# Address arithmetic and register loads moved to the front of each step, and a message sum put between the two halves of a later group's gathers

## The chip, the cores and the metric

One core of one Trainium2 chip runs the kernel. Its engines are the TensorE (PE in the profile, its weight loads PEld), the VectorE (DVE), the ScalarE (ACT), the GpSimd (POOL) and the SyncE (SP), which issues most DMAs. Each engine has a sequencer that reads its instructions in program order, works out register values itself, and hands matmuls, copies and the like on to the engine. The metric is device time in microseconds of one launch.

## The reference

A graph with 3125 nodes of 64 features and 100000 edges, sorted by destination. First a message network of three layers, then a relational network of three layers, each with a residual and a layer norm:

```python
for _ in range(3):                                   # message layers
    msg_in = jnp.concatenate([h[src], h[dst], edge_attr], axis=1)
    msg = silu(msg_in @ W1e + b1e) @ W2e + b2e
    agg = jax.ops.segment_sum(msg, dst, n) / deg
    h = h + mlp(jnp.concatenate([h, agg], axis=1), W1n, b1n, W2n, b2n)
...
for l in range(3):                                   # relational layers
    agg = segment_sum(x[src], edge_type * n + dst, 4 * n) / max(cnt, 1)
    x = x @ root + b + einsum('rni,rio->no', agg.reshape(4, n, -1), W)
```

## The kernel before

**Edges in groups.** The kernel first sorts the edges into tiles of 128 by their block of destination nodes and their span of source nodes (span of the first 1.35 ms, untouched by the change). Eight tiles (`GT = 8`) are a group, all with one destination block; there are `NG = 160` groups, and every one of the six layers goes over all of them. `places` holds, for every group, eight offsets into the table of source rows and, for the message layers, one more for the destination block.

**One step of the TensorE.** `stage(g, u, i)` is one step. The first four and the last few steps of a layer stand unrolled; the rest is a loop `Fori(1, QUADS)` of 39 passes with four steps in each, `u` being the number of the step within the pass. In the message layers (`l < LAYERS`, layers 0 to 2) a step holds: `gather_ready` (the group's one-hot matrices are there); `gather_tile` for eight tiles, three matmuls each (L934 and L935 pick the source rows out of two neighbouring parts of the table, L938 the destination row), 24 in all, into the four PSUM banks of `gat`; `turn_dst_hots`, eight transpositions of the destination one-hots (L948); `sum_messages` of the group three steps earlier, eight matmuls (L968); `load_places` for the next step (L916, nine registers out of SBUF). In the relational layers (`l >= LAYERS`, layers 3 to 5) it holds, for each of eight tiles, two gather matmuls and four sum matmuls (L977) of the group two steps earlier, 48 in all, with the load of eight registers (L918) after the fourth tile.

**Addresses.** The second operand of L934, L935 and L938 is `table_flat[:, bass.ds(register, K3)]`. Its address is worked out by the TensorE's own sequencer, in register records (`ISA` in the order, `FUSED_REGOPS` in the trace) that stand right ahead of the matmul that first needs them: two operations for L934, three for L935, two for L938, the last once a step.

**Waits.** `gat_read` says that the VectorE (the ScalarE in relational layers) has read half of `gat`; it is waited for ahead of tiles 0 and 4. The sum waits for `acc_read`, sent by the ScalarE's `keep_msums` (L714) two groups earlier, for `hot_out` (L693, the copy of the transposed one-hots), and for `low_made` of the GpSimd. On the ScalarE a step is `keep_hots` (L693, once `turned` says that the transpositions are done), `middle` (L707), `keep_msums` (L714), and `messages` (L701 and L702).

Of the kernel before, what the change touches and what calls it, by code (L numbers as in the profile page):

```python
# [18 lines left out]
GT = 8  # L19
# [3 lines left out]
K3 = 3 * HID  # L23
# [3 lines left out]
def gnn_kernel(nc, x, src, dst, edge_attr, edge_type, W1e, b1e, W2e, b2e, W1n, b1n, W2n, b2n,  # L27
# [22 lines left out]
    LAYERS = 3  # L50
# [19 lines left out]
    with ExitStack() as ctx:  # L70
# [46 lines left out]
        table_flat = table[:].rearrange("p b m k f -> p (b m k f)")  # L117
        table_next = table_flat[:, ROWW:]
# [668 lines left out]
        def _(pe):  # L787
# [100 lines left out]
            for l in range(2 * LAYERS):  # L888
# [93 lines left out]
                def stage(g, u, i, l=l):  # L982

                    known = isinstance(g, int)
                    gathers = not known or g < NG
                    off, dst_off = [], None
                    if gathers:
                        off = [pe.snap(r, min_val=0, max_val=SPAN * ROWW * (NS - 1)) for r in tile_regs[u % 2]]
                        if l < LAYERS:
                            dst_off = pe.snap(dst_reg[u % 2], min_val=0, max_val=ROWW * (NB - 1) + K3)  # L990
                        gather_ready(g, u, i)
                    if l < LAYERS:
                        if gathers:
                            for j in range(GT):
                                gather_tile(g, u, j, off, dst_off)
                            turn_dst_hots(g, u)
                        if not known or g >= LAG:
                            sum_messages(g - LAG, (u + 4 - LAG) % 4)
                        if gathers:
                            load_places(g + 1, u + 1)  # L1000
                    else:
                        adds = not known or g >= 2
                        for j in range(GT):
                            if gathers:
                                gather_tile(g, u, j, off, dst_off)
                            if adds:
                                if j == 0:
                                    sums_ready(g - 2, (u + 2) % 4)
                                sums_half(g - 2, (u + 2) % 4, j)
                            if j == 3 and gathers:  # L1010
                                load_places(g + 1, u + 1)

                load_places(0, 0)
                for g in range(4):
                    stage(g, g, 0)
# [432 lines left out]
```

## Time and profile before

| | us |
|---|---|
| median of 3 runs (lowest, highest) | 5863.55 (5863.24, 5865.77) |
| the profiled execution | 5864.59 |
| its span in the trace | 5862.9 |
| sorting of the edges and building of tables | 0 to about 1505 |
| message layer 0 | about 1505 to 2310 |
| message layers 1 and 2 | about 2350 to 3005, 3045 to 3705 |
| relational layers 3 to 5 | about 3745 to 5795 |

Busy shares of the span: PE 81%, PEld 69%, DVE 68%, POOL 58%, ACT 47%. The profile counts an engine's busy time by what the engine executes; time in which its sequencer works on registers is in no busy share, but the sequencer's records stand in the trace with the mark q (PEldq for the TensorE's). Columns of a group of instructions by line are: engine, operation, count, shortest/median/longest duration in ns, start of the first and of the last. "issue" is idle time for which the profile shows no releaser.

### The profile page before, as it was taken

To read this page: it belongs to the slowest core of one execution; us is meant where nothing else is said; L and a number is where in the kernel's file an instruction comes from. 1 tells how busy PE (TensorE), PEld (TensorE's weight loads), DVE (VectorE), ACT (ScalarE), POOL (GpSimd) and SP (SyncE) were. 2 spreads that over 40 slices of the span, in tenths; PEclk is the share of its full clock that TensorE was granted. 3 is DMA by queue.
4 is the path that set the end of the run, shared out by engine and by line. 5 is a ranking of instruction groups with operands and counts; after the bars stand their busy time and mean duration, and the time that the engine had idled before them with its cause. 6 is when DMAs were issued, how large, how long until landed. Compare 5 with 4: busy or idle time off the path is not lost.

```text
span 5862.9 us, 173813 instructions
## 1 busy us (share of the span) xinstructions
PE 4725.5 (81%) x47638; PEld 4058.5 (69%) x47639; DVE 3972.5 (68%) x9658; ACT 2755.2 (47%) x4407; POOL 3395.9 (58%) x4499
## 2 busy tenths in 40 slices
PE   2666666660577777888888888899999999999998
PEld 2444444440466665777767777699998999999997
DVE  6444444440589997777767777688875888578885
ACT  1111111112456665677757777555554555455553
POOL 0777777770367775455535555366653666446663
PEclk9755555555799999999999999899998999899997
DMA  8111111117899997777757777244432444234441
GB/s 327 29 29 29 29 29 29 29 28 244 272 312 333 334 334 245 248 264 266 264 176 265 263 265 265 92 133 133 132 120 83 132 132 133 93 109 133 132 133 58
DMA packets 358467, 975.41 MB, mean 166 GB/s; under 512 B 71168, under 2 KB 83796, under 8 KB 358411
## 3 DMA queue, kind: packets, MB, share of 16 engines
q1 hardware_dynamic: 317352, 946.00, 48.9%
q0 software_dynamic: 38400, 28.13, 2.7%
q10 hardware_dynamic: 2658, 0.51, 0.0%
q8 instruction: 37, 0.61, 0.0%
q14 instruction: 20, 0.16, 0.0%
HBM read 774.54 MB, written 199.06 MB: 166 GB/s over the span
## 4 chain that ended last, share of the span: by engine, by line
PE 56%; POOL 15%; issue 10%; DMA 9%; DVE 7%; another core or an unknown queue 2%; ACT 1%; DVEq 0%; POOLq 0%; SPq 0%; ACTq 0%
PE sums L977 21%; POOL recs L517 14%; PE gat L934 10%; PE gat L935 10%; DMA arena<-rows_d 5%; PE gat L938 4%; PE sums L968 4%; DMA arena<-recs 3%; PE sums L948 2%; DMA recs<-arena 2%; DVE arena L1341 1%; PE gat L1060 1%; DVE arena L1316 1%; DVE arena L1337 1%
## 5 line engine op out<-in xcount | busy, mean ns | idle before, releaser
L934 PE MATMUL gat<-table,arena 128*128 x7680 | 1913.4, 249 | 370.8 <-DVE arena L1341 186.7
L935 PE MATMUL gat<-table,arena 128*128 x7680 | 1916.7, 250 | 0.0
L977 PE MATMUL sums<-arena 128*128 128x192 bf16 x15360 | 1887.2, 246 | 0.0
L1357 DVE TENSOR_SCALAR arena<-iota_s,meta_t 128x512 bf16<-128x512 int16 x3840 | 1523.0, 469 | 363.2 <-PE sums L977 363.2
L977 PEld LDWEIGHTS sums<-arena 128*128 128x128 bf16 x15360 | 1325.3, 98 | 0.1
L517 POOL DMA_INDIRECT recs<-arena x800 | 949.8, 1187 | 377.4 <-issue 374.9
L721 ACT CAST arena<-gat 128x768 bf16<-128x768 f32 x960 | 767.0, 799 | 809.3 <-PE gat L935 809.3
L934 PEld LDWEIGHTS gat<-table,arena 128*128 128x128 bf16 x7680 | 747.7, 97 | 548.3 <-issue 482.1
L938 PE MATMUL gat<-table,arena 128*128 x3840 | 959.9, 250 | 0.0
L540 POOL TENSOR_TENSOR arena<-arena 128x512 bf16<-128x512 f32 x480 | 532.6, 1110 | 726.3 <-ACT arena L707 726.0
L1341 DVE TENSOR_TENSOR arena<-arena,gat 128x256 f32<-128x256 f32 x1920 | 812.0, 423 | 65.8
L935 PEld LDWEIGHTS gat<-table,arena 128*128 128x128 bf16 x7680 | 748.0, 97 | 137.2 <-issue 0.4
L592 POOL TENSOR_TENSOR arena<-arena 128x256 f32<-128x256 f32 x480 | 414.5, 864 | 656.7 <-ACT arena L729 655.9
L693 ACT COPY arena<-sums 128x1024 bf16<-128x1024 bf16 x480 | 486.3, 1013 | 518.2 <-PE sums L948 517.8
L1337 DVE TENSOR_TENSOR arena<-gat,arena 128x256 f32<-128x256 f32 x960 | 402.8, 420 | 263.4 <-PE gat L938 262.1
L832 PE MATMUL gat<-arena 25*125 25x39 bf16 x800 | 232.0, 290 | 401.8 <-DVE arena L1179 401.8
L656 ACT COPY arena<-gat 25x1000 bf16<-25x1000 bf16 x100 | 98.4, 984 | 829.8 <-PE gat L806 807.8
L832 PEld LDWEIGHTS gat<-arena 25*125 25x125 bf16 x800 | 141.2, 176 | 445.9 <-DVE arena L1179 429.7
L598 POOL TENSOR_TENSOR arena<-arena 128x256 f32 x480 | 384.6, 801 | 91.2 <-POOL arena L595 91.2
L968 PE MATMUL sums<-arena 128*128 128x192 bf16 (+1 forms) x3840 | 406.1, 248 | 11.1 <-ACT arena L714 10.9
L729 ACT COPY arena<-sums 128x768 f32<-128x768 f32 x480 | 386.2, 804 | 9.9 <-PE sums L977 9.9
L938 PEld LDWEIGHTS gat<-table,arena 128*128 128x128 bf16 x3840 | 380.3, 99 | 13.4
(184 smaller groups left out, 6228.6 us busy)
## 6 DMA issues: line engine op xcount, KB each, us to landing
arena<-hots_d SPq DMA_DIRECT2D x320, 768.0 KB, 4.5
arena<-hots_d SPq DMA_DIRECT2D x480, 512.0 KB, 3.5
arena<-recs SPq DMA_DIRECT2D x640, 272.0 KB, 3.9
hots_d<-arena SPq DMA_DIRECT2D x160, 768.0 KB, 8.1
arena<-rows_d SPq DMA_DIRECT2D x160, 512.0 KB, 6.9
recs<-arena SPq DMA_DIRECT2D x1, 43520.0 KB, 119.4
recs<-arena POOLq DMA_INDIRECT x800, 2.9
arena<-in_edge_attr_dram SPq DMA_DIRECT2D x100, 62.5 KB
```

Source lines behind the costliest of these rows:

```text
L517: pool.indirect_dma_start(recs, bass.IndirectOffsetOnAxis(ap=addr_out[s][:, j:j + 1].bitcast(U32), axis=0), rec_out[s][:, j, :], None).the ...
L540: pool.tensor_tensor(parts[u][:, :, 2 * HID:K3], left[s], parts[u][:, :, HID:2 * HID], ALU.subtract).then_inc(low_made, 1)
L693: act.copy(oh[u], oh_ps[u % 2].rearrange("p (j n) -> p j n", n=P)).then_inc(hot_out, 1)
L721: act.copy(gb[u % 4][:, 4 * h:4 * h + 4, :], gat[:, 1024 * h:1024 * h + 1024].rearrange("p (j w) -> p j w", j=4) [:, :, 0:K3]).then_inc(ga ...
L934: pe.matmul(at, ohT[u][:, 0, tile], table_flat[:, bass.ds(off[j], K3)], start=True, stop=False)
L935: ins = pe.matmul(at, ohT[u][:, 1, tile], table_next[:, bass.ds(off[j], K3)], start=False, stop=l >= LAYERS)
L938: ins = pe.matmul(at, ohT[u][:, 2, tile], table_flat[:, bass.ds(dst_off, K3)], start=False, stop=True)
L968: ins = pe.matmul(accp[u % 2][:, 0:w], oh[u][:, j, :], parts[u][:, j, 0:w], start=j == 0, stop=j == GT - 1)
L977: ins = pe.matmul(accp[s][:, 256 * r:256 * r + K3], oh4[u][:, t, r * P:(r + 1) * P], gb[u][:, t, :], start=t == 0, stop=t == GT - 1)
L1337: dve.tensor_tensor(z[s][:, tiles, :], found_parts[:, tiles, 0:HID], rec[:, tiles, 0:HID], ALU.add).then_inc(z_step, 1)
L1341: ins = dve.tensor_tensor(z[s][:, tiles, :], z[s][:, tiles, :], found_parts[:, tiles, m * HID:(m + 1) * HID], ALU.add)
L1357: ins = dve.tensor_scalar(oh4[u][:, j, :], iota_s[:], meta_t[:, bass.ds(GT * g + j, 1), PT - HID], None, ALU.is_equal)
```

## The change

In `stage`, all addresses of the step are now worked out at its front, by `pe.lower_ap` on the same operands; the matmuls then find them ready. In the message layers `load_places` for the next step follows at once, ahead of the group's wait and its gathers. And in the message layers the sum of group g - 3 stands after tiles 0 to 3; tiles 4 to 7 and the transpositions follow it. In the relational layers only the addresses move.

```diff
@@ in stage(g, u, i)
                         if l < LAYERS:
                             dst_off = pe.snap(dst_reg[u % 2], min_val=0, max_val=ROWW * (NB - 1) + K3)
+                            pe.lower_ap(table_flat[:, bass.ds(dst_off, K3)])
+                        for r in off:
+                            pe.lower_ap(table_flat[:, bass.ds(r, K3)])
+                            pe.lower_ap(table_next[:, bass.ds(r, K3)])
+                        if l < LAYERS:
+                            load_places(g + 1, u + 1)
                         gather_ready(g, u, i)
                     if l < LAYERS:
-                        if gathers:
-                            for j in range(GT):
+                        for j in range(GT // 2):
+                            if gathers:
                                 gather_tile(g, u, j, off, dst_off)
-                            turn_dst_hots(g, u)
                         if not known or g >= LAG:
                             sum_messages(g - LAG, (u + 4 - LAG) % 4)
                         if gathers:
-                            load_places(g + 1, u + 1)
+                            for j in range(GT // 2, GT):
+                                gather_tile(g, u, j, off, dst_off)
+                            turn_dst_hots(g, u)
```

TensorE, message layer 1, third step of a pass, before; the sum of the step ahead ends, the load and the copies of the registers follow, and then records and matmuls take turns:

```order
L968 MATMUL sums<-arena 128x192 x7
L916 ISA
L916 TENSOR_LOAD places
L988 ISA
L931 ISA [waits hots_loaded2]
L934 ISA [waits gat_read]
L934 MATMUL gat<-table,arena 128x192
L935 ISA
L935 MATMUL gat<-table,arena 128x192
L938 ISA
L938 MATMUL gat<-table,arena 128x192
```

The same place after; the transpositions now end the step ahead:

```order
L948 MATMUL sums<-ident_b,arena 128x128 x7
L988 ISA
L991 ISA
L994 ISA
L993 ISA x2
L994 ISA x3
L916 ISA
L916 TENSOR_LOAD places
L931 ISA [waits hots_loaded2]
L934 MATMUL gat<-table,arena 128x192 [waits gat_read]
L935 MATMUL gat<-table,arena 128x192
L938 MATMUL gat<-table,arena 128x192
```

So 17 address records of two or three operations each, spread over the step, have become seven of up to six operations in a row (L991, L994, L993 twice, L994 three times), and the wait for `gat_read` moved from a record to the matmul.

TensorE, relational layer 3, second step of a pass, before:

```order
L977 MATMUL sums<-arena 128x192 x4
L988 ISA
L931 ISA [waits hots_loaded1]
L934 ISA [waits gat_read]
L934 MATMUL gat<-table,arena 128x192
L935 ISA
L935 MATMUL gat<-table,arena 128x192
L954 REGISTER_ALU
L961 REGISTER_ALU [waits acc_read]
L977 MATMUL sums<-arena 128x192 [waits gat_read,oh_made]
```

and after:

```order
L977 MATMUL sums<-arena 128x192 x4
L988 ISA
L993 ISA
L994 ISA x3
L993 ISA x2
L994 ISA
L931 ISA [waits hots_loaded1]
L934 MATMUL gat<-table,arena 128x192 [waits gat_read]
L935 MATMUL gat<-table,arena 128x192
L954 REGISTER_ALU
L961 REGISTER_ALU [waits acc_read]
L977 MATMUL sums<-arena 128x192 [waits gat_read,oh_made]
```

Sixteen address records, two a tile, are now seven in a row ahead of the step's first matmul; the load of the registers (L918) keeps its place after the fourth tile.

## Rows read from the trace of the kernel before

**Rows 1.** Busy time by stretch: message layer 0, message layer 1, relational layer 3

```profile
core 0: us, PE busy (x) PEld busy (x) DVE busy (x) ACT busy (x) POOL busy (x), PEclk, DMA share, GB/s
1600.00:2200.00 600.00, 453.61 (x4948) 371.42 (x4949) 551.79 (x1238) 358.31 (x617) 427.21 (x739) 0.98 0.96 328
2400.00:2900.00 500.00, 441.67 (x4974) 357.50 (x4972) 382.84 (x870) 354.58 (x622) 283.47 (x499) 1.00 0.79 265
3800.00:4300.00 500.00, 500.00 (x6064) 500.00 (x6062) 403.77 (x1010) 289.96 (x379) 302.56 (x380) 1.00 0.42 132
```

**Rows 2.** TensorE's sequencer by line, 2380 to 3000 us (message layer 1)

```profile
L1016 PEldq COMPARE_BRANCH  x39: 76/208/221, 2382.0 to 2993.9; - x39
...
L916 PEldq FUSED_REGOPS  x153: 65/65/65, 2380.9 to 2992.8; - x153
L916 PEldq TENSOR_LOAD <-places x153: 836/843/867, 2381.0 to 2992.9; - x153
...
L988 PEldq FUSED_REGOPS  x114: 165/165/165, 2386.5 to 2989.9; - x114
...
L931 PEldq FUSED_REGOPS  x152: 46/46/60, 2382.7 to 2990.1; - x152
...
L934 PEldq FUSED_REGOPS  x1218: 37/37/42, 2380.1 to 2992.2; - x174
...
L935 PEldq FUSED_REGOPS  x1219: 46/51/56, 2380.0 to 2992.4; - x175
```

**Rows 3.** Order of time, PE alone, one step of message layer 1

```profile
2501.94 0.61 PE L948 MATMUL sums<-ident_b,arena 128*128 128x128 bf16 x8
2502.38 0.83 PE L968 MATMUL sums<-arena 128*128 128x192 bf16 x8
2503.57 0.25 PE L934 MATMUL gat<-table,arena 128*128 x1 [0.35 <-issue]
...
2505.82 0.28 PE L948 MATMUL sums<-ident_b,arena 128*128 128x128 bf16 x2
```

**Rows 4.** Line L916 in the same steps, 2501 to 2512 us

```profile
L916 PEldq FUSED_REGOPS  x3: 65/65/65, 2502.1 to 2509.8; - x3
```

**Rows 5.** Lines L934, L935 and L977, all that started between 3740 and 4101.92 us

```profile
L934 PEldq FUSED_REGOPS  x724: 42/42/42, 3747.1 to 4101.9; - x181
...
L934 PE MATMUL gat<-table,arena x721: 246/246/368, 3747.2 to 4101.9; 128*128 x181
...
L935 PE MATMUL gat<-table,arena x720: 246/246/368, 3747.3 to 4101.5; 128*128 x180
...
L977 PE MATMUL sums<-arena x2816: 242/246/246, 3753.6 to 4101.8; 128*128 128x192 bf16 x188
```

**Rows 6.** The loop's branch in relational layer 3, 3775 to 4378 us

```profile
L1016 PEldq COMPARE_BRANCH  x39: 76/208/215, 3775.8 to 4377.7; - x39
```

**Rows 7.** A record of six operations (GpSimd's), and loads of eight registers and of one

```profile
L582 POOLq FUSED_REGOPS  x120: 84/84/98, 3744.1 to 5781.2; - x120
...
L918 PEldq TENSOR_LOAD <-places x152: 588/592/598, 3778.0 to 4375.7; - x152
...
L547 POOLq TENSOR_LOAD <-places x480: 285/290/1572, 1543.9 to 3696.7; - x160
```

**Rows 8.** Order of time, ACT alone, the same step as in rows 3

```profile
2502.58 1.01 ACT L693 COPY arena<-sums 128x1024 bf16<-128x1024 bf16 x1 [1.19 <-PE sums L948]
2503.49 0.62 ACT L707 CAST arena<-arena 128x512 bf16<-128x512 f32 x1
2504.01 0.32 ACT L714 COPY arena<-sums 128x192 f32<-128x192 f32 x1
```

**Rows 9.** What TensorE sat idle for ahead of L968, whole span: us, times

```profile
  ACT arena L714: 23.1, 12
```

**Rows 10.** Branch and register load in message layer 0

```profile
L1016 PEldq COMPARE_BRANCH  x39: 76/208/235, 1558.7 to 2296.8; - x39
...
L916 PEldq TENSOR_LOAD <-places x161: 838/1308/3142, 1506.4 to 2295.9; - x161
```

## The prediction, made before the changed kernel ran

> **What bounds the kernel now.** I began with the busy time by stretch [rows 1]. In relational layer 3 the PE is busy for the whole 500 us with 6064 matmuls, 82.5 ns each: the array is the bound. In message layer 1 it is busy 88%, no other engine is over 77%, the clock is full. In message layer 0 the DVE is busy 92%. So layer 1 needs explaining, and its idle time has the releaser "issue" in the order of time [rows 3]: nothing that the page counts as busy holds the array back. The answer is in the sequencer's records [rows 2]. From the first branch (2382.0) to the last (2993.9) are 38 passes: 16.10 us a pass, 4.025 us a step. The array's own work in a step is 32 matmuls at 82.5 ns and eight transpositions 55 ns apart (L948 at 2501.94, L968 at 2502.38 [rows 3]): 3.08 us. The sequencer's records in a step are one load of 843 ns, records of 65, 165 and 46 ns, 17 address records of 37 to 51, and a few short ones (L954, L946, L931's addition, L957): about 2.0 us, plus what passes between records. That I take from the step's front: from L916 at 2502.1 [rows 4] to the first gather at 2503.57 [rows 3] are 1.47 us, the five records in it (65, 843, 165, 46, 42) make 1.16, so each takes some 60 ns on top. About 27 records then come to 3.6 us, a pass's end and the handing over of matmuls to the rest of the 4.025. **In message layers 1 and 2 the TensorE's sequencer is the bound**, and it is busy without a pause.
>
> **How far it runs ahead.** Where the array is slower, the sequencer gets ahead of it, and how far is to be counted [rows 5]: until 4101.92 it had begun 724 records of L934, so it had handed over 723 pairs L934 and L935, and the sums that belong to them, 4 x 723 less the 64 of the first two groups, 2828. The array had started 721 + 720 + 2816 = 4257 of these 4274 matmuls. 17 were waiting. Before the load of the next step in layer 1 only the 12 that the program order allows were waiting, so there the limit does not show. I take 17 as the most that it can be ahead. The trace sees it at one instant, so 16 to 18 stays open.
>
> **The change, sequencer first.** 17 short records (17 x (45 + 60) = 1.8 us) become seven long ones. No six-operation record is in the TensorE's trace; GpSimd's takes 84 ns [rows 7], a two-operation one of the PE's 37 to 42, a four-operation one 65 [rows 2]. I take 84, bounds 65 and 100. Seven cost 7 x 0.144 = 1.01 us. The sequencer is thus relieved of 0.8 us a step, to about 3.2. But now everything that feeds the array nothing stands in one place.
>
> **Message layers 1 and 2, the front.** Between the last transposition handed over and the next gather: copies of registers 0.225, addresses 1.01, L916 0.125, load 0.90 (the load has the same nine registers as before: one register costs 0.29, eight 0.59 [rows 7], nine 0.84, as if a second load were made for the ninth, so I don't expect it to shrink), L931 0.106: 2.37 us. What hides it is the array's backlog at that moment: one matmul just started and 17 waiting, of which eight are transpositions: 10 x 0.0825 + 8 x 0.055 = 1.27 us. The array stands still for 1.10 us. Step: 3.08 + 1.10 = 4.18, and once a pass the branch adds about 0.39 (register addition 0.09, branch 0.27, longer records 0.03), 0.10 a step: **4.28 us against 4.025**. Over 2 x 160 steps: +82 us. Bounds: records of 65 ns give 4.15 (+40), of 100 ns 4.39 (+117); 16 or 18 pairs move it by 0.08 (26 us) either way.
>
> **Message layers, the sum's place.** The sum of g - 3 now starts 1.4 us earlier in the step (four tiles and the transpositions). Of its four semaphores only `acc_read`, sent by L714, held it for more than 0.3 us in the trace of before, 12 times in all [rows 9]; it is close now, since it needs ScalarE's L693, L707 and L714 behind `turned` of the step ahead. From the last transposition's start (2501.94 + 7 x 0.055 = 2502.33) to the end of L714 at 2504.33 [rows 8] are 2.0 us. Then follow sum (0.66), four tiles (0.99) and seven transposition spacings (0.39) until the next `turned`: a ring of 4.05, with 0.05 for the semaphore 4.1. At 4.28 it costs nothing; below 4.1 it would be the bound. The DVE gets the halves of `gat` further apart (0.66 us of sum between them), but is busy 3.08 us of a step (77% of 4.025 [rows 1]), so a step of 4.28 leaves it 1.2 us to wait in.
>
> **Message layer 0.** A pass takes (2296.8 - 1558.7)/38 = 19.42 us, 4.86 a step [rows 10], and the DVE sets it. The load is slower there, 1308 ns in the middle. The PE's new cycle is 4.28 + 0.47 + 0.1 for two more records = 4.85 to 4.95, no longer well below. I take +0.12 a step, +20 us; bounds 0 (the DVE still hides it) and +50.
>
> **Relational layers.** The front is 0.225 + 6 x 0.144 + 0.106 (a last record of three operations) + 0.106 = 1.30 us; the backlog is 18 x 0.0825 = 1.485. Hidden. In the first step of a pass the branch comes on top: 0.09 + 0.27 + 0.24 + 0.97 + 0.12 = 1.69, exposed 0.20; and then two gathers (0.165) stand against three records (0.29), another 0.13. A pass of 15.84 us (3775.8 to 4377.7, 38 passes [rows 6]) gets 0.33 longer: 39 x 3 x 0.33 = **+39 us**. Bounds: at 65 ns 0.22 a pass (+25), at 100 ns 0.55 with a little in the other steps (+65).
>
> **Sum.** 5862.9 (span) + 82 + 20 + 39 = 6004. The launch was 1.7 above its span and the median of the runs 1.0 below that launch: about 6005 us, 2.4% slower.
>
> **A page against the row.** In the relational stage the sequencer was stopped at 17 matmuls ahead [rows 5]. The Trainium skill, "TensorE: Matmul & The Clock Gate", section "Architectural detail: the array is 16× 32×32, not 1× 128×128", gives the TensorE's queue 64 entries. If a weight load and a matmul take one each, an estimate by that page is 32 pairs, nearly twice the count; the row decides in my sum, and what a longer queue would bring is the first rival. The Trainium skill, "Perfetto Trace Analysis", section "Tensor Engine Instruction (MATMUL, LD_WEIGHTS)", has a waiting matmul stand in a queue while the sequencer goes on; by that the move of `gat_read` from a record to the matmul (front of the step) favours the change. No row of before shows it.
>
> **Rivals.** First, **the backlog can be deeper** than what I counted (something else stopped the sequencer at 17). It decides from about 31 pairs on, when 2.37 us are covered. Then layers 1 and 2 run at the ring's 4.05 to 4.1, (4.07 - 4.025) x 320 = +15 us, layer 0 and the relational layers as before: 5880. Against it: the limit was met where no semaphore holds the sequencer. Second, and on the other side, **the sequencer's relief shows in full**: backlog deep and `acc_read` sooner than my ring. The step falls to the sequencer's 3.2 us, 320 x 0.82 = -262: 5600, half of it 5730. For it: layers 1 and 2 are bound by that sequencer. Against it: two separate limits must both be wrong. Third, **the load no longer holds the sequencer**, since nothing behind it needs its registers at once: at 0.25 to 0.3 shorter, as with eight registers, the step is 4.10 (the ring), +24 for the two layers instead of +82: 5947. Against it: L918, whose registers nobody needs soon, has its full 592 ns too. Fourth, **layer 0 and the ring add up**: late `turned` delays ScalarE and layer 0 turns PE-bound at 5.2: 6060 to 6130. That the change doesn't do what it says is excluded by the order: no address record is left between the gathers.
>
> **How the numbers follow.** Likeliest, with its bounds (40 + 0 + 25 and 117 + 50 + 65, ends together rarely): 5935 to 6095, chance 0.72. Third rival 0.08 (inside). Deep backlog 0.08, of which 0.05 lies within 0.2% of now. Relief in full or half 0.05. Above 6095: 0.07. The range takes in most of the fourth: 5930 to 6110. A measurement of this kernel tells about 0.2%, 12 us, from no change. Faster 0.05, within 0.2% 0.05, slower 0.90.
>
> **What would show it.** Right: in layers 1 and 2 a pass of 17.1 us instead of 16.10, PE idle about 1.1 us ahead of each first gather and nowhere else, gathers 82 ns apart instead of up to 130; in the relational layers a pass of 16.2 with the idle time in its first step only. Wrong: six-operation records far from 84 ns; a load that is shorter; idle time ahead of L968 (then the ring binds, and `acc_read` is the releaser); more than 17 matmuls ahead of the array; a message layer 0 that is faster or longer than 830 us.

## The result, and the profile after

| | before | after |
|---|---|---|
| median (lowest, highest), us | 5864.45 (5863.24, 5865.77), 4 runs | 6010.3 (5988.39, 6050.96), 4 runs |
| the profiled execution | 5864.59 | 6050.96 |
| its span | 5862.9 | 6049.3 |

The changed kernel is slower: 1.0257 times the time of before, 95% interval 1.0202 to 1.0312. Its runs also lie further apart than those of before, and the profiled one is the longest of the four, 40.7 us above the median. The lines below therefore explain 186.4 us between two spans, of which 145.9 us is the difference of the medians.

Where the time went can be read from the branch that closes each loop of 39 passes: the first and the last lie 38 passes apart. TensorE's sequencer, after, the branches of message layers 0 and 1 and of relational layers 3 and 4 (columns as in rows 2):

```profile
L1023 PEldq COMPARE_BRANCH  x39: 76/208/217, 1560.1 to 2351.2; - x39
```

```profile
L1023 PEldq COMPARE_BRANCH  x39: 76/208/208, 2440.1 to 3090.3; - x39
```

```profile
L1023 PEldq COMPARE_BRANCH  x39: 76/208/216, 3914.5 to 4533.6; - x39
...
L1023 PEldq COMPARE_BRANCH  x39: 76/208/211, 4636.2 to 5251.9; - x39
```

| loop | us a pass before | after | over 38 passes |
|---|---|---|---|
| message layer 0 | 19.42 | 20.82 | +53.0 |
| message layer 1 | 16.10 | 17.11 | +38.4 |
| message layer 2 | 16.11 | 17.10 | +37.6 |
| relational layers 3, 4, 5 | 15.84 each | 16.29, 16.20, 16.20 | +17.1, +13.8, +13.8 |
| the rest (outside the 38 passes of each loop) | | | about +13 |

Busy time by stretch of the kernel after, in message layers 0 and 1 and in relational layer 3; these answer to [rows 1]:

```profile
core 0: us, PE busy (x) PEld busy (x) DVE busy (x) ACT busy (x) POOL busy (x), PEclk, DMA share, GB/s
1600.00:2200.00 600.00, 412.80 (x4688) 383.47 (x4685) 511.25 (x1172) 340.62 (x586) 414.33 (x703) 0.96 0.93 310
2400.00:2900.00 500.00, 379.62 (x4594) 358.02 (x4592) 358.65 (x814) 323.08 (x575) 239.74 (x443) 0.99 0.71 243
3900.00:4400.00 500.00, 496.21 (x5899) 482.91 (x5896) 393.65 (x984) 282.66 (x369) 294.36 (x369) 1.00 0.41 129
```

In layer 1 the array was busy 88% of the time; it is now busy 76%, and VectorE, ScalarE and GpSimd are busy for a smaller share too. Nobody works more; all wait. For whom is read from one step. The array alone, after, in order of time, the step whose sequencer records follow below (start, us, what ran, and in brackets the idle time before it and what ended it; `x8` with 0.83 us are eight matmuls that follow each other):

```profile
2605.11 0.25 PE L934 MATMUL gat<-table,arena 128*128 x1 [0.86 <-issue]
...
2606.11 0.83 PE L968 MATMUL sums<-arena 128*128 128x192 bf16 x8
2607.77 0.61 PE L948 MATMUL sums<-ident_b,arena 128*128 128x128 bf16 x8
2609.28 0.25 PE L934 MATMUL gat<-table,arena 128*128 x1 [0.90 <-issue]
```

The gathers now run at the array's pace: from 2605.11 to 2606.03 (the last one of the first half) are eleven spacings of 84 ns. All the idle time has been gathered in one piece of 0.86 to 0.90 us ahead of each first gather, with "issue" as its releaser, as the forecast put it. (The idle time counts from the end of the last transposition; from start to start the gap is longer: the last of eight transpositions, 55 ns apart, starts at 2608.16, the next gather at 2609.28, 1.12 us later, of which 0.055 would pass anyway.) In the step with the branch it is 1.38, and the trace names another releaser there:

```profile
2459.91 0.25 PE L934 MATMUL gat<-table,arena 128*128 x1 [1.38 <-DVE arena L1348]
```

The VectorE's L1348 of that step, and the sequencer's last record ahead of the gather:

```profile
2458.78 0.88 DVE L1348 TENSOR_TENSOR arena<-arena,gat 128x256 f32<-128x256 f32 x2
```

```profile
L931 PEldq FUSED_REGOPS  x1: 51/51/51, 2459.8 to 2459.8; - x1
```

L1348 was through at 2459.66, and the sequencer came to L931 only at 2459.8; the gather started at 2459.91. So here too the sequencer came last, and the name DVE is that of the last signal before it. What was waiting when such a front began is counted from all that had started on PE from 2400 us until the front of the step above began with its L988 record:

```profile
L934 PE MATMUL gat<-table,arena x365: 242/246/368, 2409.4 to 2602.7; 128*128 x183
...
L935 PE MATMUL gat<-table,arena x365: 243/246/368, 2409.5 to 2602.7; 128*128 x183
...
L938 PE MATMUL gat<-table,arena x365: 244/246/368, 2409.7 to 2602.8; 128*128 x183
...
L948 PE MATMUL sums<-ident_b,arena x360: 219/219/314, 2413.2 to 2599.9; 128*128 128x128 bf16 x180
...
L968 PE MATMUL sums<-arena x344: 243/246/248, 2422.2 to 2602.6; 128*128 128x192 bf16 x172
...
L988 PEldq FUSED_REGOPS  x36: 165/165/165, 2407.1 to 2602.8; - x36
```

The layer began at 2409.4, and 46 of its steps had been handed over: 3 x 368 gathers, 368 transpositions and, since its first three steps have no sum, 344 sum matmuls. The array had started 3 x 365, 360 and all 344. So nine gathers and eight transpositions were waiting: **17 again**, as in [rows 5], now in a message layer, where [rows 2 to 4] could not show it. From L988 at 2602.8 to the first gather at 2605.11 the front took 2.3 us.

### The profile page after: what moved, and what is told of

Its sections match the earlier page's. It is cut to its first block, busy times and chain, and to the rows that moved or that the text cites. A ratio compares the mean times of both kernels' runs of the same rounds, so it can differ in the third digit from the quotient of the medians.

```text
span 6049.3 us, 164576 instructions
## 1 busy us (share of the span) xinstructions
PE 4664.9 (77%) x47638; PEld 4168.1 (69%) x47639; DVE 3968.4 (66%) x9658; ACT 2736.2 (45%) x4407; POOL 3375.5 (56%) x4499
## 4 chain that ended last, share of the span: by engine, by line
PE 53%; POOL 15%; issue 11%; DVE 9%; DMA 8%; another core or an unknown queue 2%; ACT 0%; DVEq 0%; POOLq 0%; SPq 0%; ACTq 0%
PE sums L977 21%; POOL recs L517 14%; PE gat L934 10%; PE gat L935 9%; DMA arena<-rows_d 5%; PE gat L938 4%; PE sums L968 3%; DVE arena L1348 3%; DMA arena<-recs 2%; DVE arena L1344 2%; PE sums L948 2%; PE gat L1067 1%; DMA recs<-arena 1%; DVE arena L1322 1%
## 5 line engine op out<-in xcount | busy, mean ns | idle before, releaser
L934 PE MATMUL gat<-table,arena 128*128 x7680 | 1911.5, 249 | 611.7 <-issue 286.1
L935 PE MATMUL gat<-table,arena 128*128 x7680 | 1907.9, 249 | 0.0
L977 PE MATMUL sums<-arena 128*128 128x192 bf16 x15360 | 1888.4, 246 | 0.8
L977 PEld LDWEIGHTS sums<-arena 128*128 128x128 bf16 x15360 | 1314.1, 98 | 25.8 <-issue 24.8
L934 PEld LDWEIGHTS gat<-table,arena 128*128 128x128 bf16 x7680 | 758.6, 99 | 721.6 <-issue 398.9
L1348 DVE TENSOR_TENSOR arena<-arena,gat 128x256 f32<-128x256 f32 x1920 | 811.8, 423 | 65.9
L693 ACT COPY arena<-sums 128x1024 bf16<-128x1024 bf16 x480 | 486.4, 1013 | 803.8 <-PE sums L948 803.8
L935 PEld LDWEIGHTS gat<-table,arena 128*128 128x128 bf16 x7680 | 759.6, 99 | 1.7
L968 PE MATMUL sums<-arena 128*128 128x192 bf16 (+1 forms) x3840 | 420.0, 253 | 22.0 <-ACT arena L714 21.0
L938 PEld LDWEIGHTS gat<-table,arena 128*128 128x128 bf16 x3840 | 382.2, 100 | 1.3
```

Of the source, the lines that this page charges most:

```text
L693: act.copy(oh[u], oh_ps[u % 2].rearrange("p (j n) -> p j n", n=P)).then_inc(hot_out, 1)
L934: pe.matmul(at, ohT[u][:, 0, tile], table_flat[:, bass.ds(off[j], K3)], start=True, stop=False)
L935: ins = pe.matmul(at, ohT[u][:, 1, tile], table_next[:, bass.ds(off[j], K3)], start=False, stop=l >= LAYERS)
L938: ins = pe.matmul(at, ohT[u][:, 2, tile], table_flat[:, bass.ds(dst_off, K3)], start=False, stop=True)
L968: ins = pe.matmul(accp[u % 2][:, 0:w], oh[u][:, j, :], parts[u][:, j, 0:w], start=j == 0, stop=j == GT - 1)
L977: ins = pe.matmul(accp[s][:, 256 * r:256 * r + K3], oh4[u][:, t, r * P:(r + 1) * P], gb[u][:, t, :], start=t == 0, stop=t == GT - 1)
```

## The experiments

All of them leave the relational layers as they were before; only the message layers differ, and a pass of message layer 1 is what tells the theories apart. The theory: two things bound a step, a **block** of sequencer work against a backlog of 17 matmuls, and a **ring** from the transpositions through ScalarE's L693, L707 and L714 back to the sum, 4.1 us long once the sum stands between the halves. A block is a stretch of register work in which the sequencer hands the array nothing; the backlog is what the array has been handed and has not yet started. The main rivals: the slowdown is all the sum's place; it is the register load; or it is the address records themselves.

| kernel (message layers) | median, us | ratio to before, 95% | layer 1, us a pass | layer 0 |
|---|---|---|---|---|
| before (four batches) | 5861.7 to 5863.7 | 1 | 16.10 | 19.42 |
| changed, relational undone | 5951.87 | 1.0146 (1.0129 to 1.0163) | 17.11 | 19.96 |
| addresses at the front only | 5948.61 | 1.0160 (1.0134 to 1.0186) | 17.06 | 19.52 |
| sum between the halves only | 5935.67 | 1.0119 (1.0102 to 1.0136) | 16.87 | 19.61 |
| changed, load after the sum | 6102.64 | 1.0412 (1.0394 to 1.0429) | 18.56 | 20.59 |
| addresses at the front, load after the gathers | 5766.35 | 0.9833 (0.9816 to 0.9849) | 14.84 | 19.43 |
| change in layer 0 only | 5885.58 | 1.0046 (1.0018 to 1.0073) | 16.10 | 19.89 |
| load after the gathers only | 5868.55 | 1.0009 (1.0000 to 1.0019) | 16.10 | 19.55 |
| changed, load ahead of the transpositions | 5915.0 | 1.0087 (1.0071 to 1.0104) | 16.66 | 19.51 |
| the same, ScalarE's `keep_msums` first | 5783.48 | 0.9867 (0.9850 to 0.9883) | 14.93 | 19.69 |
| changed, `keep_msums` first | 5950.15 | 1.0148 (1.0131 to 1.0165) | 17.06 | 19.61 |
| load after the sum, `keep_msums` first | 5632.48 | 0.9609 (0.9596 to 0.9622) | 13.09 | 19.52 |

**The relational part undone.** The message layers as in the change; the addresses of the relational layers stay between their gathers:

```diff
                             pe.lower_ap(table_flat[:, bass.ds(dst_off, K3)])
-                        for r in off:
-                            pe.lower_ap(table_flat[:, bass.ds(r, K3)])
-                            pe.lower_ap(table_next[:, bass.ds(r, K3)])
                         if l < LAYERS:
+                            for r in off:
+                                pe.lower_ap(table_flat[:, bass.ds(r, K3)])
+                                pe.lower_ap(table_next[:, bass.ds(r, K3)])
                             load_places(g + 1, u + 1)
```

> The message layers as in the changed kernel, the relational layers as before. My theory (address records at the front of a relational step are covered by the backlog except in a pass's first step) says that undoing them gives back about 45 us, what the three relational layers grew by: passes of 15.84 us again instead of 16.17 to 16.29, and the message layers unchanged at 17.1 us a pass; about 5965 us. If the relational growth came from something else (the clock, later starts), the passes stay at 16.2.

5951.87 us (5944.23 to 5966.76). Relational passes are back at 15.84, layer 1 stays at 17.11. The two parts of the change can be told apart: the 45 us of the three relational loops belong to the block of addresses there. The total lies 13 us below the expected 5965; the runs of this kernel are 23 us apart themselves.

**Addresses alone.** The addresses at the front, load and sum where they were:

```diff
                             dst_off = pe.snap(dst_reg[u % 2], min_val=0, max_val=ROWW * (NB - 1) + K3)
+                            pe.lower_ap(table_flat[:, bass.ds(dst_off, K3)])
+                            for r in off:
+                                pe.lower_ap(table_flat[:, bass.ds(r, K3)])
+                                pe.lower_ap(table_next[:, bass.ds(r, K3)])
                         gather_ready(g, u, i)
```

> Message layers: addresses at the front of the step, but the load of registers and the sum of messages where they were before; relational layers as before. My theory (the sequencer feeds the array nothing for 2.3 us in a row, and the backlog of 17 matmuls covers 1.27) sees the same block here: load, copies and addresses follow each other at the end of one step and the front of the next. Layers 1 and 2: 17.1 us a pass, as in the changed kernel. The rival (the sum's new place, held by acc_read, is what costs) says 16.1 or less.

The branches of layer 1 with the addresses alone:

```profile
L1021 PEldq COMPARE_BRANCH  x39: 76/208/215, 2384.7 to 3033.1; - x39
```

(3033.1 - 2384.7)/38 = 17.06. The load stands at the end of the step before anyway, so load and addresses form the same block, and the pass is as long as with the whole change, 17.11. Neither the sum's place nor the load's few lines of movement are needed for the slowdown.

**The sum alone.**

```diff
-                            for j in range(GT):
+                            for j in range(0, 4):
                                 gather_tile(g, u, j, off, dst_off)
-                            turn_dst_hots(g, u)
                         if not known or g >= LAG:
                             sum_messages(g - LAG, (u + 4 - LAG) % 4)
                         if gathers:
+                            for j in range(4, 8):
+                                gather_tile(g, u, j, off, dst_off)
+                            turn_dst_hots(g, u)
+                        if gathers:
                             load_places(g + 1, u + 1)
```

> Only the sum moved between the halves; addresses and load where they were before, relational layers as before. The ring from turned over ScalarE's L693, L707 and L714 back to the sum (2.01 + 0.07 + 0.66 + 0.99 + 0.39 = 4.12 us) should set layers 1 and 2: 16.5 us a pass, with idle time ahead of L968. If the ring is not there, the sequencer keeps them at 16.1; if the sum's place is the whole cost, 17.1.

16.87, more than the 16.5 expected. The waits of this kernel, 2500 to 3000 us (engine and line, what it waited for: us in total, times, longest):

```profile
PEld sums L968 <- ACT arena L714: 27.0, 89, 0.3
...
PE gat L934 <- issue: 61.2, 117, 0.9
```

The ring is there: in 89 of some 119 steps, three in four, the sum waits for L714. Those steps take 4.12 us; the first step of a pass takes 4.5, since there the branch lengthens the block. So the ring is real and costs 0.8 us a pass when only the sum moves, but it is a second limit under the first: it does not reach 17.1, and the addresses alone, which leave it open, do.

**The load behind the sum.** With the relational part undone, `load_places` is taken out of the front:

```diff
                             sum_messages(g - LAG, (u + 4 - LAG) % 4)
                         if gathers:
+                            load_places(g + 1, u + 1)
+                        if gathers:
                             for j in range(4, 8):
```

> Message layers as in the changed kernel, but the load of the next step's registers stands after the sum, between the halves, instead of at the front; relational layers as before. The front shrinks from 2.27 to 1.26 us, which the backlog of 1.27 covers. By the sequencer and the array alone a step would take 3.3 us (13.2 a pass); by the ring over acc_read 4.12, 16.5 a pass. I expect 16.5, and idle time ahead of L968. If the cost of the change did not lie in the front's length, it stays 17.1.

**Missed, by two us a pass.** 18.56 instead of 16.5, and 6102.64 us, the slowest of all. The wait ahead of the sum (2500 to 3000 us) of this kernel:

```profile
PE sums L968 <- ACT arena L714: 79.6, 108, 0.8
```

I had taken the load as free behind a queue of matmuls. It isn't, because the sequencer does not go past a sum whose semaphore has not come. That can be seen in the kernel after, at the step above. L957, the record right ahead of the sum, and L931's addition, the first record behind the sum:

```profile
L957 PEldq EVENT_SEMAPHORE  x1: 51/51/51, 2605.2 to 2605.2; - x1
```

```profile
L931 PEldq ALU_OP  x1: 32/32/32, 2606.1 to 2606.1; - x1
```

and ScalarE's L714 of the same step:

```profile
2604.29 1.01 ACT L693 COPY arena<-sums 128x1024 bf16<-128x1024 bf16 x1 [1.36 <-PE sums L948]
2605.20 0.62 ACT L707 CAST arena<-arena 128x512 bf16<-128x512 f32 x1
2605.72 0.32 ACT L714 COPY arena<-sums 128x192 f32<-128x192 f32 x1
```

L714 ends at 2606.04, the sum starts at 2606.11, and the next record of the sequencer, L931's addition, stands at 2606.1: 0.9 us after L957. Where the semaphore had come (the first kernel with `keep_msums` first, below) the same two records are 0.1 us apart:

```profile
L957 PEldq EVENT_SEMAPHORE  x1: 51/51/51, 2702.9 to 2702.9; - x1
```

```profile
L931 PEldq ALU_OP  x1: 32/32/32, 2703.0 to 2703.0; - x1
```

So a load behind the sum starts only when the ring has closed, and becomes part of it: 2.01 from the last transposition to the end of L714, 0.07 for the semaphore, 1.13 for the load and its two short records (0.12 + 0.90 + 0.09 and the way to the array), 0.99 for four tiles, 0.39 for the transpositions: 4.6 a step, 18.4 a pass. The Trainium skill, "Perfetto Trace Analysis", section "Tensor Engine Instruction (MATMUL, LD_WEIGHTS)", has such a matmul wait in a queue while the sequencer goes on; these rows show the opposite, and the miss came from reckoning as if it were so.

**The load between gathers and transpositions, the sum at the end.** Addresses at the front as in the experiment with the addresses alone, and:

```diff
                                 gather_tile(g, u, j, off, dst_off)
+                        if gathers:
+                            load_places(g + 1, u + 1)
                             turn_dst_hots(g, u)
                         if not known or g >= LAG:
                             sum_messages(g - LAG, (u + 4 - LAG) % 4)
-                        if gathers:
-                            load_places(g + 1, u + 1)
```

> Message layers: addresses at the front; the load of the next registers between the last gather and the transpositions, where 17 matmuls (1.4 us) stand ahead of the array to cover its 1.03 us; the sum at the step's end, as before, where acc_read has long come. Relational layers as before. Theory: no block of the sequencer is longer than the backlog and the ring is open, so layers 1 and 2 fall from 16.10 us a pass to what array and VectorE allow, 3.2 to 3.6 us a step, 13 to 14.4 a pass; layer 0 stays at 19.4 (VectorE). Total 5864 - 320 x 0.6, about 5670 us (5610 to 5740). If the load or the addresses hold the array wherever they stand, layers 1 and 2 stay at 16.1 or above.

Faster than before, by 1.7%: 5766.35 us, 14.84 a pass. The relief of the sequencer that the change was able to bring is thus real: 17.06 with the addresses alone becomes 14.84 when the load leaves the block. It fell short of the expected 13 to 14.4 a pass (5610 to 5740 us), and the waits (2500 to 2900 us) name the VectorE, which has to read the half of `gat` before the array may write it again:

```profile
PEld gat L934 <- DVE arena L1346: 44.1, 81, 0.9
```

That name is right for a part only. The array alone, in one step and at the start of the next:

```profile
2600.97 0.26 PE L934 MATMUL gat<-table,arena 128*128 x1 [0.19 <-DVE arena L1346]
...
2602.17 0.62 PE L948 MATMUL sums<-ident_b,arena 128*128 128x128 bf16 x8
...
2604.10 0.25 PE L934 MATMUL gat<-table,arena 128*128 x1 [0.65 <-DVE arena L1346]
```

At 2600.97 the VectorE was late: its read of the second half ended at 2600.91, and the gather started 0.06 us later. At 2604.10 it was not. The gathers there need the first half only, which L1346 had read by 2602.17; what came last was the sequencer, whose last record ahead of the gather ended at 2604.05, behind a block of some 1.8 us with the branch in it. The transpositions at 2602.17 start 0.28 us after the last gather, behind the load. Added up from the starts on PE over these 400 us, a pass loses about 2.5 us against the array's own work: about 1.4 ahead of the first gathers, 0.4 ahead of the transpositions, both by the sequencer, and 0.6 by the VectorE.

**The load alone**, moved to the same place, with the addresses left between the gathers (the diff above, and nothing else; the addresses stay between the gathers):

> Message layers: only the load of the next registers moved, to the place that it has in e5 (between the last gather and the transpositions); addresses interleaved with the matmuls and the sum at the end, as before; relational layers as before. My theory takes the sequencer's record total for the bound as long as the addresses are 17 short records: the place of the load then changes nothing, 16.1 us a pass, 5864 us. If e5's gain came from the load's place alone, 14.8.

5868.55 (5864.96 to 5876.32), 10 runs, 1.0009 (1.0000 to 1.0019), 16.10 a pass. With this the two moves of layer 1 stand as a square: neither 16.10, load alone 16.10, addresses alone 17.06, both 14.84. While the sequencer is bound by its amount of work, the load's place is worth nothing; once the amount has fallen, it is worth 2.2 us a pass. The gain is in neither move alone.

**Layer 0 alone.** The whole change for `l == 0`:

```diff
-                        if l < LAYERS:
+                        if l == 0:
                             load_places(g + 1, u + 1)
```

and likewise for the addresses and the sum.

> The whole change in message layer 0 alone, all other layers as before. In the changed kernel's profile layer 0 took 5.20 us a step instead of 4.86, where I had forecast +0.12. Theory: the TensorE's cycle there is now about 4.9 us, as long as VectorE's, so every slow load and every drop of the granted clock adds: 5880 to 5920 us, with runs that differ by more than before's 2.5. If layer 0's growth came from the state that the other layers leave or from the whole kernel's clock, it is gone: 5864.

5885.58 (5859.49 to 5923.72) over 10 runs, against 5863.68 (5854.12 to 5869.51) over 13 of before: +22, with a spread four times as wide. A message layer 0 with the change is sometimes as fast as before and sometimes 60 us slower. The time lies in the expected 5880 to 5920 us; what the kernel after shows of the reason stands below: of the two that were expected, the lowered clock is borne out, and a cycle of the TensorE as long as the VectorE's is not.

**The load ahead of the transpositions, the sum in the middle.**

```diff
                             for j in range(4, 8):
                                 gather_tile(g, u, j, off, dst_off)
+                            load_places(g + 1, u + 1)
                             turn_dst_hots(g, u)
```

> Message layers: the change with one line moved, the load of the next registers stands between the last gather and the transpositions instead of at the front; the sum stays between the halves; relational layers as before. The front falls from 2.27 to 1.26 us, under the backlog of 1.27, and the load, other than in e4, stands behind 17 matmuls and not right behind the sum's wait. What is left is the ring over acc_read: 2.01 + 0.07 + 0.66 + 0.99 + 0.39 = 4.12 us a step, 16.5 a pass, idle time only ahead of L968; 5896 us. If the load costs wherever it stands, 17.1 or more.

16.66 a pass (5915 us, 19 more than expected), three steps at the ring's 4.12 and a first one of 4.30, counted from sum to sum. But idle time "only ahead of L968" was wrong; the waits, 2500 to 2900 us:

```profile
PE gat L934 <- issue: 46.0, 96, 0.9
...
PE sums L968 <- ACT arena L714: 23.7, 72, 0.3
```

The front still shows in every step, 0.34 us in three of four. In those three it costs nothing, since the sum waits for L714 afterwards all the same: the ring sets the step, and the block is hidden in it. Against the kernel with the load at the same place and the sum at the end (14.84), the sum's place costs 1.8 us a pass.

**The ring cut.** If the ring is the limit, it must give way on ScalarE. `keep_msums`, which sends `acc_read`, needs nothing of this step's `turned`; it can stand ahead of `keep_hots`:

```diff
                         for u in range(4):
+                            keep_msums(4 * i + u - 4, u)
                             keep_hots(4 * i + u, u)
                             middle(4 * i + u - 1, (u + 3) % 4)
-                            keep_msums(4 * i + u - 4, u)
                             messages(4 * i + u, u)
```

> e8, and on the ScalarE the copy that frees the sum's PSUM (keep_msums, L714) stands ahead of the copy that waits for the transpositions (keep_hots, L693) instead of behind it and middle. acc_read then no longer hangs on turned of the step ahead, and the ring is open. Theory: passes fall from e8's 16.5 to what the VectorE's reading of gat allows, as in e5: 14 to 15; 5690 to 5770 us. If the ring is not what holds e8, nothing changes.

14.93, and no wait for L714 is left. The pass is in the expected 14 to 15, the time 13 us above the expected range. But the VectorE, that I had expected as the next limit, is not it (2500 to 2900 us):

```profile
PE gat L934 <- issue: 49.5, 107, 0.9
```

It is the block again: with the load just ahead of the transpositions the array catches up during it, so that at the next front only 12 matmuls are queued (four gathers and eight transpositions), not 17: when L988 started at 2701.53, the array had started eight of the twelve gathers ahead of the transpositions. It is the 0.34 us that were there with the ring closed too.

The same line on the change itself:

> The change in the message layers (load at the front, as in e1), relational layers as before, and the ScalarE's order of e9. The ring is open here too, but I say that the changed kernel is held by the front (2.27 us against a backlog of 1.27), not by the ring: 17.1 us a pass as in e1, about 5950 us. If the ring was the real bound, the pass falls below 16.

5950.15 us, 17.06 a pass. Cutting the ring takes 0.05 us off a pass of the changed kernel, no more: the block holds it at 4.12 to 4.17 in three steps and 4.65 in the first, and with the ring cut they are 4.13 and 4.66. And the same line on the slowest of all, the load behind the sum:

> e4 (load right behind the sum, between the halves), which ran at 18.56 us a pass, with e9's order on the ScalarE (keep_msums first). Theory: in e4 the load stood behind the sum's wait for acc_read, so it was a part of the ring (2.01 + 0.07 + load and records 1.13 + 0.99 + 0.39 = 4.6 us a step). With acc_read early the wait is over before the sequencer comes to it; then 17 matmuls stand ahead of the array both at the load and at the front, better spread than in e9, where only 12 did at the front. Array 3.09 us and about 0.1 for the branch, if the VectorE can follow: 13.2 to 14.8 us a pass, 5640 to 5770 us, below e9 (14.93) and perhaps below e5 (14.84). If the load holds the array in that place by itself, it stays above 16.

**5632.48 us (5630.43 to 5633.66), 0.9609 (0.9596 to 0.9622): faster than both kernels**, and 8 us below the expected range. One line on another engine turns +4.1% into -3.9%. What that line does to the kernel before, alone, was not run. The branches of layer 1, the wait that is left (2500 to 2900 us) and the busy time by stretch:

```profile
L1024 PEldq COMPARE_BRANCH  x39: 76/208/208, 2381.4 to 2878.7; - x39
```

```profile
PE gat L934 <- issue: 10.5, 29, 0.4
```

```profile
2450.00:2900.00 450.00, 428.39 (x5317) 411.68 (x5315) 405.01 (x926) 380.48 (x675) 331.61 (x546) 0.98 0.91 315
```

13.09 us a pass, 3.27 a step, where the array's own work is 3.08. The array is busy 95%, the DVE 90%. The 29 waits are one a pass, in the step with the branch; in the other steps load and addresses are two blocks, each shorter than the backlog. One step of it, the array alone, and the line of the load in the same stretch, 2598 to 2606 us:

```profile
2601.48 0.61 PE L948 MATMUL sums<-ident_b,arena 128*128 128x128 bf16 x8
2601.94 0.25 PE L934 MATMUL gat<-table,arena 128*128 x1
...
2602.93 0.83 PE L968 MATMUL sums<-arena 128*128 128x192 bf16 x8
2603.62 0.26 PE L934 MATMUL gat<-table,arena 128*128 x1
```

```profile
L916 PEldq TENSOR_LOAD <-places x2: 841/843/845, 2599.1 to 2602.3; - x2
```

The load behind the sum starts at 2602.3, when the array has not yet begun that sum (2602.93), and ends before the array is through with it; the gathers follow without a gap.

## Why the prediction was right, and where it was not

The forecast was 6005 us, slower; the median is 6010.3. The mechanism of its largest term held in every part that was tested. That the total came within 5 us is partly luck, since the errors of the other terms are larger than that. Term by term:

**Layers 1 and 2, +82.** The loops gave +38.4 and +37.6, over 38 passes each, +78 for 39 (+82 was for 40); a pass of 17.12 was forecast, 17.11 measured. Records of six operations were taken at 84 ns, from GpSimd [rows 7], and take 74 on the TensorE. The changed kernel's sequencer, layer 1, one of the seven of the front, and the load of the registers:

```profile
L991 PEldq FUSED_REGOPS  x154: 74/74/74, 2431.8 to 3086.2; - x154
```

```profile
L916 PEldq TENSOR_LOAD <-places x153: 837/843/862, 2432.9 to 3083.1; - x153
```

That makes the front 2.28 us (2602.835 to 2605.11) and 2.32 (2606.96 to 2609.28) instead of 2.37. The gaps that show are 1.03 and 1.07 from start to start (1.12 less 0.055 for the second) where 1.10 was forecast; the backlog covered 1.25 of each, 1.27 was forecast, and the errors nearly cancel. Three steps of a pass take 4.12 to 4.17, the first 4.65, so the branch costs 0.50 where 0.39 was forecast, and the other steps 4.15 where 4.18 was. The ring was as near as the forecast had it: L714 ended at 2606.04, and the sum started at 2606.11, one spacing after the last gather. It would have begun to bind within another 0.1 us.

**Layer 0, +20.** Measured +53 in the profiled execution and +22 over ten runs of the kernel with layer 0 alone. The size was near, the step behind it was wrong: it said that the PE's cycle becomes as long as the DVE's. Passes at the full clock are as long as before: 19.3 us on average in the kernel after (23 of its 38 passes), 19.2 in the one before (28 of 38). Two stretches with the full clock, one of each kernel (before first):

```profile
1850.00:1900.00 50.00, 36.81 (x413) 29.75 (x413) 48.17 (x105) 30.98 (x54) 37.93 (x65) 1.00 0.96 332
```

```profile
1850.00:1900.00 50.00, 35.23 (x432) 33.38 (x430) 44.61 (x110) 31.25 (x53) 38.51 (x65) 1.00 0.97 342
```

The kernel after starts 432 matmuls in 50 us, before 413. Over all such stretches of layer 0 at 1.00 the two are even (415 matmuls after and 418 before, on average): with the full clock the change costs layer 0 nothing. Now stretches with the clock lowered for part of the time (before first, then two of after):

```profile
1600.00:1650.00 50.00, 39.28 (x391) 33.06 (x392) 41.63 (x97) 27.81 (x47) 31.87 (x55) 0.90 0.94 308
```

```profile
2000.00:2050.00 50.00, 31.51 (x320) 29.07 (x320) 39.75 (x84) 24.63 (x45) 29.26 (x50) 0.89 0.87 280
2250.00:2300.00 50.00, 34.98 (x360) 32.11 (x360) 40.24 (x89) 25.29 (x46) 30.24 (x53) 0.90 0.84 268
```

At 0.90 and 0.89 before still starts 391 matmuls, after 360 and 320. Cut at the branches, ten passes of before had a lowered clock, none under 0.91, and took 20.1 us on average (18.0 to 21.8). Of after, five passes at 0.92 or 0.93 took 22.0 (20.6 to 23.7) and nine at 0.80 to 0.88 took 24.2 (22.6 to 25.5). The 53 us stand in these fourteen passes: the clock was lowered more often, and a fall cost more. Ahead of this fall, in the kernel after, the array had stood still for 2.77 us. The granted clock then was 0.50, that is 1.2 GHz in place of 2.4, for about 3.4 us from 2124.4 on, and the sum takes 1.51 us instead of 0.85:

```profile
2123.32 0.25 PE L934 MATMUL gat<-table,arena 128*128 x1 [2.77 <-DVE arena L1323]
...
2124.36 1.51 PE L968 MATMUL sums<-arena 128*128 128x196 bf16 x8
```

That the array's lost time was hidden behind the DVE before, and comes on top now because the front leaves no slack, fits these rows; it is argued, not shown by a run of its own. What decides when and how often the clock falls stays open. The lowered clock is the likeliest reason for the wider spread of the runs, since the spread appears with the change in layer 0 alone. The forecast had named a message layer 0 of more than 830 us as a sign of being wrong, and the profiled execution has it: from its first gather (1519.4) to its last sum (2361.0) are 842 us, against 787 before. In the execution with layer 0 alone they are 803.

**Relational layers, +39.** A pass of 16.17 was forecast; 16.29, 16.20 and 16.20 came, +45 in the loops. (Every pass of layer 3 is the 0.09 longer; why is not known.) The array in layer 3 at the start of a pass (the branch stands at 4110.03), after:

```profile
4111.69 0.26 PE L934 MATMUL gat<-table,arena 128*128 x1
4111.78 0.25 PE L935 MATMUL gat<-table,arena 128*128 x1
4112.01 0.50 PE L977 MATMUL sums<-arena 128*128 128x192 bf16 x4
```

The last sum ahead started at 4111.32, so the front shows 0.29 us (0.37 less a spacing of 0.0825) where 0.20 was forecast, and the gap behind the two gathers 0.14 (0.13 forecast). Both stand in a pass's first step only. The undone relational part confirms the whole term.

**The rest.** Some 13 us stand outside the 38 passes of the loops. From its first gather to its last sum each layer grew by what its loop did, to 2 us in all; the other 11 us lie between the layers and at both ends of the program, were not in the sum at all, and their cause stays open. Against the forecast the profiled execution thus has -6 in layers 1 and 2 (76 in the passes counted), +33 in layer 0, +6 in the relational layers and +13 here, which is 6051 rather than 6005. If the median run differs from it in layer 0 alone, layer 0 cost it about 12, not 53, and -6, -8, +6 and +13 happen to leave 5 us.

**Rivals.** A deeper backlog: excluded, 17 were counted again, with transpositions among them. The relief in full: not in the change, but the kernels with the load elsewhere show that it was there to be had (5632 us where the rival said 5600), and that it took just the two things that the rival named, a block that is covered and `acc_read` ahead of the ring. A shorter load: excluded, the load in layer 1 still took 843 ns, with nothing close behind it that needs its registers. Layer 0 and ring together at 5.2 a step: the profiled execution has that mean (20.82 a pass) and, at 6051, lies just under the rival's 6060, but not by the rival's way. Most passes are at 4.8 a step as before, and the mean comes from those with a lowered clock; in the median the rival's time is not reached.

## What to carry to other kernels

An engine's sequencer can bound a kernel in which no busy share is over 90%; list its records, add what passes between them (about 60 ns each here, worked out from the five records of a step's front), and compare with the step. Less work in one block can be slower than more work spread out: no run of records between two matmuls may be longer than what the array has queued, and a register load goes behind many queued matmuls that wait for nothing, not behind a wait. When a consumer is moved forward in the step, follow its semaphore around through the other engines, since shortening that ring (`keep_msums` ahead of `keep_hots`) can be what turns the move from a loss into a gain.

## What the runs showed of the hardware that was not expected

- TensorE's sequencer stands still at a matmul whose semaphore has not come, and does no register work behind it (0.9 us between L957 and L931's addition, against 0.1 where it had come).
- It hands over at most 17 matmuls more than the array has started, in message and in relational layers alike.
- A fused record of six operations takes 74 ns on the TensorE's sequencer and 84 on GpSimd's.
- A name in the waits can be that of the last signal and not of what came last: ahead of a gather whose semaphore had long come, the gather started 0.06 us after the sequencer's last record (2604.05 to 2604.10 with `DVE` named).
- In message layer 0 passes with a granted clock of 0.91 to 0.93 took 20.1 us on average in one order of the work (ten passes) and 22.0 in the other (five).
